# Eight-core transformer layer: dependent work queued later, weight casts in quarters, output weights by column blocks

## The reference

```python
q = rope(x @ wq)                       # 16 heads of 128
k, v = rope(x @ wk), x @ wv            # 4 heads, each used by 4 heads of q
p_g = softmax(causal(q @ k.T / sqrt(128)))
p_l = softmax(local(q @ k.T / sqrt(128)))     # a window that starts 128 before each block of 256
x1 = layernorm(x + (0.5 * (p_g @ v + p_l @ v)) @ wo)
x_ln = layernorm(x1) * gamma + beta
logits = l2norm(x_ln) * scale @ l2norm(mu)    # 16 experts x 128 slots
dispatch = softmax(logits, over tokens); combine = softmax(logits, over slots)
slot_in = dispatch.T @ x_ln
h = gelu(slot_in @ W1[e] + b1); slot_out = h @ W2[e] + b2
out = layernorm(x1 + combine @ slot_out)
```

## Time and profile before

| what | us |
|---|---|
| median of 3 timed runs (lowest, highest) | 4011.46 (3873.94, 4350.87) |
| the profiled execution, slowest core | 3864.06 |
| its span, first to last instruction, core 0 | 3862.5 |
| spans of the 8 cores | 3825.3 to 3862.5 |
| PE busy | 3435.6 (89%) |
| ACT busy | 1440.4 (37%) |
| DVE busy | 1421.7 (37%) |
| POOL busy | 470.0 (12%) |

### The profile page before, as it was taken

How to read it: one execution, slowest core, us unless ns; L and a number is a source line. 1 busy time by engine, 2 the same in 40 slices (tenths; PEclk the granted TensorE clock), 3 DMA queues, 4 the chain that set the end, 5 groups by cost and what they waited for, 6 DMA issues and landing times.

```text
span 3862.5 us, 66120 instructions; the slowest of 8 cores (3825.3 to 3862.5 us)
## 1 busy us (share of the span) xinstructions
PE 3435.6 (89%) x24864; PEld 2108.2 (55%) x24864; DVE 1421.7 (37%) x3203; ACT 1440.4 (37%) x2020; POOL 470.0 (12%) x673
## 2 busy tenths in 40 slices
PE   7778778988896878987978799999999999999998
PEld 4335445656554445555555555677744455777543
DVE  1444445454442454543555522111144322111244
ACT  2443445566552444554655432211111222211111
POOL 1131112122110122121132200000000000000000
PEclk9989899999997988988999999999999999999999
DMA  9797676456437776694354420366786200767743
GB/s 177 191 214 153 134 172 139 129 148 117 120 109 146 195 180 166 169 127 133 110 131 116 155 97 33 135 247 235 269 310 217 109 34 34 249 242 262 280 153 134
DMA packets 142744, 624.64 MB, mean 162 GB/s; under 512 B 18400, under 2 KB 22496, under 8 KB 119904
## 3 DMA queue, kind: packets, MB, share of 16 engines
q1 hardware_dynamic: 109056, 423.26, 32.5%
q0 software_dynamic: 15520, 114.30, 19.6%
q10 hardware_dynamic: 17856, 82.85, 5.8%
HBM read 612.99 MB, written 188.75 MB: 208 GB/s over the span
## 4 chain that ended last, share of the span: by engine, by line
PE 71%; DMA 10%; DVE 7%; ACT 5%; issue 5%; POOL 1%; ACTq 0%; DVEq 0%; SPq 0%; POOLq 0%
PE ob L1182 12%; PE sc L1092 11%; PE pr L494 9%; PE pr L405 9%; PE sc L1387 6%; PE sc L597 4%; PE ob L625 4%; DMA AR<-mu_t 3%; PE pr L1387 3%; PE ob L1387 3%; PE sc L1233 3%; ACT AR L375 2%; DMA AR<-xT_r 2%; ACT AR L601 2%; PE pr L437 1%
## 5 line engine op out<-in xcount | busy, mean ns | idle before, releaser
L601 ACT ACTIVATE AR<-sc 128x1024 bf16<-128x1024 f32 (+2 forms) x640 | 561.5, 895 | 422.3 <-PE sc L597 403.4
L405 PE MATMUL pr<-AR 128*128 128x512 bf16 x2560 | 641.1, 391 | 68.4 <-DMA AR<-xT_r 21.2
L494 PE MATMUL pr<-AR 128*128 128x512 bf16 x2048 | 528.4, 395 | 38.7 <-DMA AR<-wo 18.3
L1182 PE MATMUL ob<-AR 128*128 128x256 bf16 x4096 | 459.6, 273 | 0.0
L1092 PE MATMUL sc<-AR 128*128 128x512 bf16 x2048 | 452.5, 379 | 0.0
L625 PE MATMUL ob<-AR 128*128 128x129 bf16 x3840 | 311.1, 226 | 154.2 <-DVE AR L671 88.1
L1182 PEld LDWEIGHTS ob<-AR 128*128 128x128 bf16 x4096 | 399.4, 98 | 54.6
L405 PEld LDWEIGHTS pr<-AR 128*128 128x128 bf16 x2560 | 243.6, 100 | 312.6 <-issue 106.3
L597 PE MATMUL sc<-AR 128*128 128x256 bf16 (+1 forms) x2304 | 358.1, 279 | 61.9 <-ACT AR L601 55.0
L625 PEld LDWEIGHTS ob<-AR 128*128 128x128 bf16 x3840 | 258.6, 101 | 242.9 <-issue 187.4
L610 POOL TENSOR_TENSOR AR<-AR 128x256 bf16<-128x256 bf16 x256 | 184.9, 722 | 1376.0 <-ACT AR L601 1216.3
(11 more groups left out here) (96 smaller groups left out, 3790.6 us busy)
## 6 DMA issues: line engine op xcount, KB each, us to landing
AR<-w_c SPq DMA_DIRECT2D x256, 512.0 KB, 6.7
AR<-wqkv_c SPq DMA_DIRECT2D x160, 512.0 KB, 5.5
w_c<-W_r POOLq DMA_DIRECT2D x32, 2048.0 KB, 20.3
AR<-x SPq DMA_DIRECT2D x32, 1024.0 KB, 6.9
x1sp<-AR ACTq DMA_DIRECT2D x32, 1024.0 KB, 5.7
AR<-b SPq DMA_DIRECT2D x32, 1024.0 KB, 10.2
AR<-x1sp SPq DMA_DIRECT2D x32, 1024.0 KB, 5.8
out<-AR ACTq DMA_DIRECT2D x32, 1024.0 KB, 4.4
```

The costliest lines, as they stand in the source:

```text
L405: tm = p.pe(lambda e, b=b, c=c, w=w, xt=xt: e.matmul(out=pr[b], lhsT=w[:, c * 128:(c + 1) * 128], rhs=xt[:, c * 512:(c + 1) * 512], start= ...
L494: tm = p.pe(lambda e, b=b, h=h, dg=dg, nt=nt, i=i: e.matmul(out=pr[b], lhsT=oT[i % 2][:, nt, h, :], rhs=wo[h][:, dg * 512:(dg + 1) * 512], ...
L601: ta = p.act(lambda e, b=b, eb=eb, lo=lo, hi=hi: e.activation(out=eb[:, lo:hi], in_=sc[b][:, 0:hi - lo], func=AF.Exp), tm, t_E_pe[h % 2])
L1182: tm = p.pe(lambda e, b=b, s=s, c=c, n=n, gp=gp: e.matmul(out=ob[b][:, s * 256:(s + 1) * 256], lhsT=rx[n][:, c * 128:(c + 1) * 128], rhs=E ...
```

## The change

1. **Ticks.** Rope's products and sum go from 2 and 3 ticks to 6 and 8; in `ln1` bias 2 to 3, apply 3 to 9, the second norm 44 and 46 to 46 and 48, stats 49 to 57, store 52 to 54, reload 58 to 62; in `mu_item` 1 and 3 to 4 and 6. `out_item` ticks until its row of x has been queued for loading.
2. **Casts.** `precast` moves a quarter of one expert's W1 or W2. Of 128 quarters, 88 (experts 0 to 10) are spread over windows 2 to 13 by a load that grows with w, up to 0.9 of a window; the other 40 are recorded in threes behind the logits' blocks 0 to 13 of the first sequence. The slab loads wait for the semaphore of their expert's casts.
3. **Output weights.** The 16 DMAs of wo now take four heads' rows by 512 columns each; four of them make one block of columns with its own semaphore, and an output product waits for its own block.

```diff
-            after(2, products)
-            after(3, total)
+            after(6, products)
+            after(8, total)
...
-                    t_wo[0], t_oT[i, h // 2], pr_free[b], inc=h == NH - 1)
+                    t_wo[dg], t_oT[i, h // 2], pr_free[b], inc=h == NH - 1)
...
+            while (i, nt) not in t_yx:
+                tick()
...
-            for n_, fn in ((1, power), (2, bias), (3, apply), (44, lambda: second(0)),
-                           (46, lambda: second(1)), (49, stats), (52, store), (58, reload)):
+            for n_, fn in ((1, power), (3, bias), (9, apply), (46, lambda: second(0)),
+                           (48, lambda: second(1)), (57, stats), (54, store), (62, reload)):
...
-            after(1, square)
-            after(3, more)
+            after(4, square)
+            after(6, more)
...
-            e_ = j // 2
-            src, dst = ((d_w1, d_w1c), (d_w2, d_w2c))[j % 2]
-            t_w12.append(p.dma("gpsimd", "D_pre", dst[e_], src[e_]))
+            e_, k = j // 8, j % 8
+            src, dst = ((d_w1, d_w1c), (d_w2, d_w2c))[k // 4]
+            t_w12[max(e_, NPRE - 1)] = p.dma("gpsimd", f"D_pre{max(e_, NPRE - 1)}",
+                                             dst[e_, k % 4], src[e_, k % 4])
...
-                    if h in (3, 5, 7, 9, 11):
-                        yield ("wo", {3: (12, 14), 5: (8, 10), 7: (0,), 9: (4,), 11: (6,)}[h])
+                    if h in (4, 6, 8, 10):
+                        yield ("wo", h // 2 - 2)
...
-        for j in range(32):
-            pre_at[2 + j * 12 // 32].append(j)
+        load = [0.0 if i < 2 or i > 13 else 28 + 7 * (i % 8) for i in range(16)]
+        for j in range(NPRE * 8):
+            i = next(i for i in range(16) if sum(load[:i + 1]) > (j + 0.5) / (NPRE * 8) * sum(load))
+            pre_at[i].append(j)
...
+                    dg = it[1]
+                    for h in (12, 8, 0, 4):
+                        t_wo[dg] = p.dma(
+                            "gpsimd", f"D_wo{dg}",
+                            v(WO + h * 4096, BF16, 8192).rearrange("p (h c) -> p h c", h=4)[
+                                :, :, dg * 512:(dg + 1) * 512],
+                            d_wo[h * 128:(h + 4) * 128, dg * 512:(dg + 1) * 512].rearrange(
+                                "(h p) c -> p h c", p=128),
...
-                if pre and min(fa, fp) >= 0.7 * (1 - len(pre) / len(pre_at[i])):
+                if pre and min(fa, fp) >= 0.9 * (1 - len(pre) / len(pre_at[i])):
...
+                if el == 0:
+                    for j in range(NPRE * 8 + n * 3, min(NE * 8, NPRE * 8 + n * 3 + 3)):
+                        precast(j)
```

More of the change, by code:

```diff
@@ L456, in q_item @@
             yield from qk_item(G, 8 + h)
-        t_wo = [None]
+        t_wo = [None] * 4
         t_oT = {}
@@ L549, in store @@
                 t_xl[el, n] = t_xl_st[0]
-                t_y_free[nt] = [t_xl_st[0], tok["m"]]
             def reload():
+                t_y_free[nt] = [t_xl[el, n], tok["m"]]
                 if i < 15:
                     load_y(i + 1, nt)
-            for n_, fn in ((1, power), (2, bias), (3, apply), (44, lambda: second(0)),
-                           (46, lambda: second(1)), (49, stats), (52, store), (58, reload)):
+            for n_, fn in ((1, power), (3, bias), (9, apply), (46, lambda: second(0)),
+                           (48, lambda: second(1)), (57, stats), (54, store), (62, reload)):
                 after(n_, fn)
@@ L840, in build_program @@
                 tick()
-        t_w12 = []
+        t_w12 = {}
+        NPRE = 11
         def precast(j):
-            e_ = j // 2
-            src, dst = ((d_w1, d_w1c), (d_w2, d_w2c))[j % 2]
-            t_w12.append(p.dma("gpsimd", "D_pre", dst[e_], src[e_]))
+            e_, k = j // 8, j % 8
+            src, dst = ((d_w1, d_w1c), (d_w2, d_w2c))[k // 4]
+            t_w12[max(e_, NPRE - 1)] = p.dma("gpsimd", f"D_pre{max(e_, NPRE - 1)}",
+                                             dst[e_, k % 4], src[e_, k % 4])
         def items_of(i):
@@ L959, in proj_stream @@
                 elif kind == "wo":
[L960 to L963, removed]
+                    dg = it[1]
[6 more added lines that the diff above has]
+                                "(h p) c -> p h c", p=128),
+                            t_x0_pe[0] if h >= 12 else [[t_w_pe[x], t_w_st[x]]
+                                                        for x in range(h, h + 4)])
+                    if dg == 3:
                         p.dma("gpsimd", "D_gb", gamv, d_gam.partition_broadcast(128))
@@ L1074, in first_phase_done @@
             return t_a_end
-        t_w12_all = t_w12[-1]
         t_etst = [t_att_end]
@@ L1166, in load_w @@
                 w_tok[k] = p.dma("sync", f"D_sl{k % 10}", slab[k % 10], src, t_sl_pe[k % 10],
-                                 t_w12_all)
+                                 t_w12[max(e_, NPRE - 1)])
             for k in range(10):
```

## The result

| | before | after |
|---|---|---|
| lowest of 4 timed runs, us | 3860.23 | 3812.23 |
| median of those runs, us | 3942.70 | 3817.23 |
| spans of the 8 cores, us | 3825.3 to 3862.5 | 3760.5 to 3810.6 |
| PE busy, us | 3435.6 | 3404.9 |
| POOL busy, us | 470.0 | 529.0 |

A forecast was written before the change was run, and what follows sets the result against it. TensorE's idle time and low clock bound the first stage (545 us to win), nothing the logits. Idle 135, three quarters 101, plus clock 46 make 147; less 80 in the logits, 67: 3864 to 3797 us, range 3700 to 3890.

The forecast's parts named there:

- L383 under 150: Sign in the first stage: VectorE's wait before the rope product L383 falls from 398.7 to under 150 us.
- no ordinary transfer of windows 2 to 13 takes over 20 us: Sign in the first stage: with casts in quarters, other transfers there land within 20 us; x1sp took 40.69 before.
- About 2% is what a measurement of this kernel can tell from no change, here 77 us: Threshold for the whole time: differences within 77 us count as no change, given chance 0.52; faster 0.41, slower 0.07.
- (a): Rival, logits: the bursts of casts cost nothing, a store passing in a turn or two; time 3717 us, chance 0.18.
- the forecast's own range: Whole time: 3757 to 3837 us around the forecast of 3797, chance 0.50.
- a turn is 3.7: Casts beside the logits: one packet per queue in turn, 3.7 us a turn, giving stalls of 11 and 65 us.
- (c): Rival, logits: bursts run at 5 us a turn and the first stage gives only 60; time 3945 us, chance 0.07.
- rope's ticks, 57 − 5: First stage: queuing rope later removes 57 us of TensorE's waits on evacuations; later q and k cost 5.
- layernorm and squares, 17: First stage: later layernorm apply and squares on ScalarE take 17 of TensorE's 55 us of waits on exponentials.
- casts in quarters, 56: First stage: quarters delay other transfers by one turn; x1sp gains 16, wqkv_c 18, mu_t 22, sum 56 us.
- output weights, 10: First output product's 18.26 us wait: needing only the first 4 loads, issued an item earlier, gains 10 us.
- (b): Rival, first stage: waits are mostly evacuation itself and exponentials, so the gain is 88 us; time 3856, chance 0.25.

The follow-up runs named there:

- the paced pairs: Changed kernel with 32 quarters in pairs behind the 16 logits blocks, each waiting for its block's last matmul; ratio 0.9628 against before, median 3713.56 us.

## Why the prediction was right and wrong

**Right: the mechanism and the sum.** First stage 148.6 against 147, logits 88 against 80, net 60.5 as a mean over the cores against 67, profiled executions 52 apart (3864.06 and 3812.23). That 148.6 falls so near 147 is luck: one execution's A isn't known to a few us, and the terms were off by more (below). Most signs were met too: window 8 under 80 us (76.7 as a mean of 8), L383 under 150 (110.4), ScalarE's long wait of "some 80 us" 88.6. One sign failed: "no ordinary transfer of windows 2 to 13 takes over 20 us". On core 5 seven did (36 did on the slowest core before), the longest load of wqkv_c among them with 26.4 us and a store of inv_c with 36.8.

**Wrong: "About 2% is what a measurement of this kernel can tell from no change, here 77 us".** This is the step that failed. By it the net of 67 us was called no change, and "within 2%" got the highest chance, 0.52. The measured ratio, 0.9867, is clear of no change: its interval is 0.982 to 0.9914, half a per cent to either side, some 18 us. A forecast of 67 us less is 1.7%, over three times that. The prediction shows no row for its 2%. The only spread that it names, 3873.94 to 4350.87, it had set aside for the sum, since it forecast an undisturbed execution; the threshold for the same execution then had to come from how closely those agree. By its own cases faster should have had what lies between 3700 and some 3845: nearly all of (a) and of the forecast's own range.

**Wrong in size: "a turn is 3.7", and one packet of each queue in a turn.** I divided 86.7% of 33 us by all 133 packets of q0. But 3.83 MB at 33 KB a packet are 117; the other 16 carry next to nothing. That makes 3.9 us for a cast's piece, and the other stretch of the same rows, all pieces, 4.7. The argument against rival (c), "under 4.2 us a turn", has the same miscount: 33 us over 7.3 pieces an engine are 4.5. In the changed kernel, core 5, 2230 to 2250, in the middle of the second burst:

```profile
q0 software_dynamic: 128, 2.10, 97.2%
q1 hardware_dynamic: 128, 0.46, 8.3%
```

2.10 MB are 4 pieces of 33 KB on each of 16 engines, so 5.0 us for each (20 us over 4). 0.46 MB of q1 are 7 pieces of 4 KB on each engine: 1.75 for one of q0, not 1. The bound at 5 us with one for one was put at 141 (36 and 105; worked like the forecast's 11 and 65 it comes to some 31 and 98). The measured 108.4 on this core lies between it and the 76 of stalls in the forecast: longer turns lengthen a stall, and more pieces of SP's queue for each turn shorten it. The 4 us of low clock beside them rest on no row. Both stalls came out larger: 33.3 for 11, 75.1 for 65 (ScalarE's two waits are 46.8 and 88.6, where some 25 and 80 were expected).

**The rule of the Trainium skill.** The Trainium skill, "DMA: Bandwidth & Descriptors", section "Queues, rings and completion order", says that an engine takes a whole packet, typically 9 to 17 descriptors, from one queue before the next. By it, as the prediction read it, the logits would have lost nothing and the time would be that of rival (a). The trace disagrees, with the two rows above and with stores of 8 pieces an engine that took 29.1 to 53.5 us in the first burst.

**Terms of the first stage** (predicted idle time × 3/4 × (1 + 170/375), so that they compare with A; each measured alone, on top of before):

| part | predicted | measured |
|---|---|---|
| rope's ticks, 57 − 5 | 57 | 37.6 |
| layernorm and squares, 17 | 19 | 56.4 (60.9 on cores 0 to 5) |
| both | 75 | 62.1 |
| casts in quarters, 56 | 61 | 60.7, with all 128 in this stage |
| output weights, 10 | 11 | 8.8, unresolved |
| all | 147 | 148.6 |

"Of the 55 us on exponentials I take 17" was the term most off. It took L526 for harmless, because ScalarE's waits in front of it came "mostly when nothing urgent was behind"; the exponentials' wait fell to 30.2 with these ticks and to 46.8 with rope's, and the waits on the copy L689, which the prediction doesn't name, went with it. No run parts L526 from the squares (L744) and the other deferred pieces. "They are issued an item earlier", gain 10, was too large: the wait went from 19.2 to 16.6 us as a mean of 8, and to 13.2 alone.

The parts alone sum to 131.6 (ticks 62.1, quarters 60.7, weights 8.8). That isn't to be held against 148.6, since the quarters alone had all 128 casts in this stage and the changed kernel has 88. The kernel that has all three parts and all 128 casts there is the one with none beside the logits, and its A is 133.6 us earlier on cores 4 to 7 (where the parts alone sum to 111); by mean spans, as above, the parts give 66, 52 and 7, and the whole 132. So the whole is no less than its parts, and no loss of a quarter among them is to be seen; whether it is more isn't settled. The other 15 or so of the 148.6 come with the 40 quarters that left the stage, which the prediction had not priced apart. The sum came out right because these errors cancelled, not because each term was.

**The rivals.** (a), bursts that cost nothing, 3717: refuted as a forecast (88 us), though the paced pairs reach that time. (b), a gain of 88: refuted by A. (c), turns of 5 us and a gain of 60: its turn was right, its first stage wrong.

## What to carry to other kernels

A wait is worth what TensorE still sees of it, and work that waits early in an in-order queue can hold up several kinds of work behind it (here ScalarE's exponentials and its copies L689), so time each part alone and with its neighbours, in more than one execution. What background transfers cost here went by the row in which they are queued and by the size of their pieces more than by their bytes: tie each to a step of the work that it runs beside (88 us became none here at two for each block, 24 at three). And set the chance of "no change" by the interval that such a comparison gives (half a per cent here), not by a round figure.

## What the runs showed of the hardware

- While casts of 33 KB pieces stand in one queue, a DMA engine takes 3.9 to 5.0 us for each in the stretches shown, and lets through 0.75 to 1.75 pieces of 4 KB of SP's queue for each of them. At the end of the second burst, core 5, the last eight casts landed 2.8 us apart; why is open.
- A store of 8 pieces an engine took 29.1 to 53.5 us in the row of 15 casts, 48.7 to 95.3 behind six loads of its own queue in the row of 25, some 12.5 behind three casts, and 2.7 alone.
- With 4 KB pieces in the cast queue the first of these took 13.1 to 14.3 us, the second 32.8 to 44.1. Smaller pieces didn't slow the casts enough to be seen in the whole (A 2051.0 and 2052.6).
- An issue of 25 casts keeps GpSimd's queue for 12 us (core 5, 2172.65 to 2184.69), while the last of them lands 108.3 us after its issue, so their place in the instruction order doesn't space them in time.
